# Gate products from the residual rows, with the norm's weight in the gate matrix and its row factor on the difference of the logits

## The reference

```python
x = o @ wo + residual
residual = x
h = rmsnorm(x, ff_ln_w)            # x * rsqrt(mean(x*x) + eps) * w
ht = h.reshape(-1, Dx)
logits = ht @ gate_w               # 256 x 8
top_vals, top_idx = jax.lax.top_k(logits, K)      # K = 2
gates = jax.nn.softmax(top_vals, axis=-1)
for e in range(E):                 # E = 8
    we = jnp.sum(gates * (top_idx == e), axis=-1)
    ye = jax.nn.silu(ht @ w1[e]) * (ht @ w3[e]) @ w2[e]
    out = out + we[:, None] * ye
```

## Time and profile before

| | us |
|---|---|
| median of three runs | 618.45 |
| lowest, highest | 615.74, 618.65 |
| profiled execution | 618.01 |
| its span | 616.2 |
| TensorE busy | 504.7 (82%) |
| VectorE busy | 499.4 (81%) |
| ScalarE busy | 362.0 (59%) |
| POOL busy | 242.5 (39%) |

### The profile page before, as it was taken

The page is one execution under the profiler, slowest core; times in us unless marked ns, Lnnn a source line. Parts: engine busy times, 40 slices in busy tenths (PEclk is TensorE's granted clock), DMA queues, the critical chain, the costliest instruction groups (busy, mean ns, idle before and its releaser), DMA issues.

```text
span 616.2 us, 10966 instructions
## 1 busy us (share of the span) xinstructions
PE 504.7 (82%) x3893; PEld 408.5 (66%) x3893; DVE 499.4 (81%) x978; ACT 362.0 (59%) x769; POOL 242.5 (39%) x208
## 2 busy tenths in 40 slices
PE   2017766799999999999669999999999999357893
PEld 1002323478788878888448999999999999223462
DVE  4999986599988888886638979989999899458894
ACT  3344435588887778776217556574565455437772
POOL 3253245644444445540653185442333510360012
PEclk9999888899999999999979999999999999788897
DMA  8300004000230000000269798899769751130001
GB/s 257 150 1 0 1 0 136 2 2 2 77 104 2 2 1 10 27 1 2 70 244 361 273 330 197 275 280 322 272 244 337 283 108 69 51 104 0 8 25 38
DMA packets 36531, 71.87 MB, mean 117 GB/s; under 512 B 5276, under 2 KB 21916, under 8 KB 36220
## 3 DMA queue, kind: packets, MB, share of 16 engines
q10 hardware_dynamic: 15280, 40.77, 20.0%
q1 hardware_dynamic: 18123, 22.26, 10.7%
q0 software_dynamic: 3072, 8.14, 5.2%
HBM read 66.03 MB, written 5.12 MB: 115 GB/s over the span
## 4 chain that ended last, share of the span: by engine, by line
PE 49%; DVE 30%; issue 7%; ACT 6%; DMA 3%; another core or an unknown queue 2%; SPq 1%; ACTq 1%; POOL 0%; DVEq 0%; POOLq 0%
PE pb L454 10%; PE pw L454 8%; PE sc L520 6%; PE pt L706 5%; PE po L454 5%; PE pb L706 4%; PE sc L706 4%; PE pt L531 3%; DVE areg L1341 2%; DVE areg L1723 2%; DVE areg L1325 2%; DVE areg L1323 2%; DVE areg L1312 1%; DVE rs L1779 1%
## 5 line engine op out<-in xcount | busy, mean ns | idle before, releaser
L1929 POOL TENSOR_TENSOR breg<-breg,con 128x512 f32<-128x512 f32 x36 | 46.9, 1302 | 89.6 <-ACT breg L956 89.6
L454 PE MATMUL pb<-areg,wreg 128*128 128x512 f16 x240 | 63.5, 406 | 14.3 <-ACT breg L956 13.0
L964 ACT ACTIVATE breg<-breg,mx 128x128 f32<-128x128 f32 (+1 forms) x128 | 56.7, 447 | 3.2 <-DVE mx L1467 3.2
L454 PE MATMUL pw<-areg 128*128 128x256 f16 x406 | 56.5, 273 | 1.4 <-DVE areg L1730 1.4
L1115 ACT CAST areg<-areg 128x512 f16<-128x512 f32 (+1 forms) x46 | 25.9, 565 | 49.3 <-DVE areg L1716 46.8
L706 PE MATMUL pb<-areg,wreg 128*128 128x128 f32 x448 | 52.7, 275 | 0.6 <-issue 0.6
L706 PEld LDWEIGHTS pb<-areg,wreg 128*128 128x128 f32 x448 | 51.3, 192 | 0.9 <-issue 0.8
L454 PEld LDWEIGHTS pb<-areg,wreg 128*128 128x128 f16 x240 | 22.9, 102 | 42.7 <-ACT breg L956 14.2
L706 PE MATMUL pt<-areg,wreg 128*128 128x128 f32 x424 | 49.9, 275 | 1.3 <-DMA wreg<-in_L_ffn_w 1.3
L706 PEld LDWEIGHTS pt<-areg,wreg 128*128 128x128 f32 x424 | 48.5, 192 | 1.6 <-DMA wreg<-in_L_ffn_w 1.5
L706 PE MATMUL sc<-areg,wreg 128*128 128x128 f32 x416 | 49.0, 275 | 0.0
(11 more groups left out here) (261 smaller groups left out, 1262.9 us busy)
## 6 DMA issues: line engine op xcount, KB each, us to landing
wreg<-in_L_ffn_w ACTq DMA_DIRECT2D x40, 896.0 KB
wreg<-in_L_ffn_w SPq DMA_DIRECT2D x14, 896.0 KB
ys_dram<-areg ACTq DMA_DIRECT2D x23, 128.0 KB
wreg<-in_L_ffn_wq SPq DMA_DIRECT2D x1, 2048.0 KB, 8.9
wreg<-in_L_ffn_wo SPq DMA_DIRECT2D x1, 2048.0 KB, 8.1
areg<-in_fside_BxSxS ACTq DMA_DIRECT2D x4, 256.0 KB, 5.7
x_in<-in_x SPq DMA_DIRECT2D x4, 256.0 KB, 4.3
h_dram<-areg SPq DMA_DIRECT2D x8, 128.0 KB
```

The lines of the kernel that those rows point to most:

```text
L454: last = nc.tensor.matmul(bank, w(a), m(b), start=first and k == 0, stop=final and k == 2)
L964: last = nc.scalar.activation(pr[:, parity, b, o:o + w], pr[:, parity, b, o:o + w], ACT.Exp, bias=mx[:, parity, k:k + 1], scale=-1.0, accu ...
L1929: G.tensor_tensor(t2[:, parity, :].rearrange("p (b n) -> p b n", b=2), t2[:, parity, :].rearrange("p (b n) -> p b n", b=2), rope_sin.rearr ...
```

## The change

The gate products are made from the residual rows. Per row, the norm is a positive factor; it is left out of the logits, whose order it doesn't change, and multiplied into the difference of the two largest before the exponential. The norm's weight per feature is multiplied into the gate matrix once, in step 16 of attention, from a new load `fflnc` at the start. The normalised rows, which only the experts still need, are made beside: for tiles 4 to 7 by ScalarE (row factor) and POOL (weight), in place of VectorE; for tiles 0 to 3 as before. The squares of tiles 4 to 7 stand behind the copies. The transposes of tiles 0 to 3 move one step earlier, and their copies with them; ten filler matmuls become four. The three VectorE instructions for the gate values stand behind the row numbers. Half of POOL's gathers of gate rows go behind its first two tile gathers.

```diff
+                sp.dma_start(fflnc[:, :], t["L0_ffn_ff_ln_w"].rearrange("(c p) -> p c", p=P)).then_inc(s["norm_in"], 16)
...
             def route_transposes(i):
-                pe.wait_ge(s["h2_ready"], i + 1)
+                pe.wait_ge(s["x1a_done"], i // 2 + 1)
...
-                    last = nc.tensor.transpose(route_bank(i)[:, c * P:(c + 1) * P], h2[:, i, c * P:(c + 1) * P], ident)
+                    last = nc.tensor.transpose(route_bank(i)[:, c * P:(c + 1) * P], x0[:, i, c * P:(c + 1) * P], ident)
...
+                if QU + 1 <= u < QU + 5:
+                    route_transposes(u - QU - 1)
                 if u >= QU + 2:
-                    route_transposes(u - QU - 2)
-                if u >= QU + 3:
-                    route_products(u - QU - 3)
+                    route_products(u - QU - 2)
...
-            route_products(NT // 2 - 1)
-            keep_clock(pt2[:, 1, :], 10)
+            keep_clock(pt2[:, 1, :], 4)
...
-                if u >= QU + 2:
-                    copy_h2T(u - QU - 2)
+                if u == H:
+                    for c in range(C):
+                        nc.scalar.activation(gate_w[:, c, :], gate_w[:, c, :], ACT.Copy, scale=fflnc[:, c:c + 1]).then_inc(s["gate_folded"], 1)
+                if QU + 1 <= u < QU + 5:
+                    copy_h2T(u - QU - 1)
...
+            for i in range(NT // 2, NT):
+                copy_h2T(i)
             for i in range(NT // 2, NT):
                 squares_of_tile(i)
             for i in range(NT // 2, NT):
-                copy_h2T(i)
+                act.wait_ge(s["rstd2_ready"], i // 2 + 1)
+                nc.scalar.activation(h2[:, i, :], x0[:, i, :], ACT.Copy, scale=ssq[:, 2, i:i + 1]).then_inc(s["h2_scaled"], 1)
...
-            for i in range(4, NT):
-                second_norm(i)
...
-            dve.sem_inc(s["d_ready"], 1)
-
-            dve.wait_ge(s["ge_ready"], 1)
-            link(V.tensor_scalar(gts[:, :, 2], gts[:, :, 1], 1.0, None, ALU.add))
-            link(V.reciprocal(gts[:, :, 3], gts[:, :, 2]))
-            link(V.tensor_tensor(gts[:, :, 4], gts[:, :, 3], gts[:, :, 1], ALU.mult))
+
+            dve.wait_ge(s["rstd2_ready"], NT // 2)
+            V.tensor_tensor(gts[:, :, 0], gts[:, :, 0], ssq[:, 2, :], ALU.mult).then_inc(s["d_ready"], 1)
...
+            dve.wait_ge(s["ge_ready"], 1)
+            link(V.tensor_scalar(gts[:, :, 2], gts[:, :, 1], 1.0, None, ALU.add))
+            link(V.reciprocal(gts[:, :, 3], gts[:, :, 2]))
+            link(V.tensor_tensor(gts[:, :, 4], gts[:, :, 3], gts[:, :, 1], ALU.mult))
...
-            gather_rows("L1_ffn_w_gate")
+            pool.wait_ge(s["norm_in"], 64)
+            pool.wait_ge(s["h2_ready"], 4)
+            for i in range(4, NT):
+                pool.wait_ge(s["h2_scaled"], i - 3)
+                G.tensor_tensor(h2[:, i, :], h2[:, i, :], ffln[:, :], ALU.mult).then_inc(s["h2_ready"], 1)
+            gather_rows("L1_ffn_w_gate", 0, NI // 2)
...
-            gather_tiles(0, 1, 2, 3)
+            gather_tiles(0, 1)
+            gather_rows("L1_ffn_w_gate", NI // 2, NI)
+            gather_tiles(2, 3)
```

More of the change, by code:

```diff
@@ L169, in build @@
         ffln = sb("ffln", [P, D])
+        fflnc = sb("fflnc", [P, C])
         wu = sb("wu", [P, 4, C])
@@ L466, in _ @@
             pe.wait_ge(s["con_in"], 16)
-            pe.wait_ge(s["norm_in"], 48)
+            pe.wait_ge(s["norm_in"], 64)
             pe.wait_ge(s["hlo_done"], 2)
@@ L566, in route_products @@
                     pe.wait_ge(s["max_done"], QU)
+                    pe.wait_ge(s["gate_folded"], C)
                 for c in range(C):
@@ L944, in hidden_high @@
                 last.then_inc(s["hi_done"], 1)
-            act.wait_ge(s["norm_in"], 48)
+            act.wait_ge(s["norm_in"], 64)
             HH = HD // 2
@@ L1974, in _, with gather_rows @@
             pool.wait_ge(s["didx_in"], 16)
-            def gather_rows(name):
-                for c in range(NI):
+            def gather_rows(name, first, last):
+                for c in range(first, last):
                     G.indirect_dma_start(out=rows[0:IQ, c * D:(c + 1) * D], out_offset=None, in_=t[name],
@@ L2008, in _ @@
             pool.wait_ge(s["rq_ready"], 1)
-            gather_rows("L1_ffn_w_up")
+            gather_rows("L1_ffn_w_up", 0, NI)
             gather_tiles(7, 8)
```

4 lines of the change are left out of this document (2 added, 2 removed).

## The result

| | before | after |
|---|---|---|
| median of 12 runs, us | 619.10 | 622.36 |
| lowest, highest | 615.74, 620.78 | 620.31, 627.02 |
| span of the profiled execution | 616.2 | 620.5 |
| ratio to before, 95% interval | | 1.0067 (1.0047 to 1.0088) |

The change is slower: 0.67% by the ratio of the runs, 3.3 us between the two medians. The forecast was 617.6 in 613.7 to 621.6.

The account below looks back on a forecast made before the run. TensorE and VectorE, busy four fifths of 616.2 us, were taken to bound it through a chain of waits. Terms -1.86 + 1.0 + 0.3 = -0.56 gave 617.45 from 618.01, or 617.9 by the median; forecast 617.6, range 613.7 to 621.6.

Parts of the forecast that it names:

- End of attention: Last head unit: ScalarE's earlier copy delays the exponentials 0.95, and the last output projection ends 0.57 late.
- Gate products: Tiles 4 to 7: no wait for the norm and fewer fillers start transposes 1.86 earlier, the 0.57 delay included.
- the clock of the rival: Rival: with fewer fillers TensorE falls to the 0.50 clock for the four-tile ladder, 3.3 more, 620.9; chance 0.05.
- Gate values and normalised rows beside: Router: moving tiny instructions taken as 0, root factors in time with 0.6 to spare, nobody waits for the stored rows.
- The lock: Router chain: POOL's multiplies block VectorE's two-input instructions through shared ports; cost taken as 1.0, bounds 0 and 3.2.
- Three collisions at half a multiply, 0.35 each: Router chain: how the cost of POOL's multiplies to VectorE was sized, 1.05, taken as 1.0.
- Gathers moved: Start of the expert stage: gate-row gathers behind tile gathers cost 0.3, within bounds 0 and 3.3.
- I take 0.3, since both have slack of about that size: Expert stage: the cost taken for weights landing later and POOL's recurrence parts moving later together.
- 0.9 at most: Second expert tile: delay of the expert weights' load by 0.36 MB more moving beside it at 408 GB/s.
- recurrence parts holding VectorE's work: Expert stage: POOL's recurrence parts, moved later to end about 327, hold VectorE's two-input work, up to 2.4.
- waits whose releaser the profile does not know: Rival: unexplained waits, ScalarE's at 362.82 and VectorE's at 546.73, may go or come: 613.9 or 621; chance 0.17.
- POOL becomes the bound: Rival: POOL from 301.4 to 328 stops the mask chain, holds VectorE's work and delays weights, 622.7; chance 0.13.

Follow-up runs that it names:

- rows_early: Changed kernel with four gate-row gathers issued at the end of attention, the other four ahead of the tile gathers; 618.73 us, ratio 0.9989 to the kernel before.
- thin_rows: Changed kernel whose second four gate-row gathers take 8 rows each instead of 88, the rest left out; 619.31 us, one execution.
- y_pause: `folded` with POOL waiting after eight of the 16 gathers of experts' results for VectorE's first dense scale; 615.08 us, ratio 0.9924 to the kernel before.
- broken_run: Changed kernel with POOL's 3.9 us recurrence arithmetic moved between the second gate-row gathers and tile gather 2; 625.91 us, ratio 1.0115 to the kernel before.
- before_again: The kernel before, unchanged, run once more for a second profile; 613.40 us, one execution.
- folded: `rows_early` without POOL's multiplies, the norm's weight multiplied in ScalarE's copy of the gathered tiles; 617.33 us, ratio 0.9977 to the kernel before.
- after_again: The changed kernel, unaltered, run once more for a second profile; 623.19 us, one execution.

## Why the prediction was wrong, point by point

*End of attention.* Right in kind, a little small: +0.85 for +0.57 (the copy ahead of the exponentials). The part for the subtraction itself, 284.48 to 285.4, was close; that TensorE would win back 0.35 of it by the end of attention was not so.

*Gate products.* Right. Predicted 1.86 earlier with the 0.57 in it; measured 2.34 less 0.85, 1.49. The ladder had the same length in both profiles, though in the second the granted clock was 0.83 in 298 to 300 and 0.50 in 300 to 302, so the clock of the rival did fall there, and cost the ladder nothing.

*Gate values and normalised rows beside.* Right: L1569 took 0.16 and had its root factors in time, and the first tile gather waited for row numbers.

*The lock.* Right in mechanism, mis-sized. The step that failed is "Three collisions at half a multiply, 0.35 each": the chain met four multiplies back to back, and each of four mask instructions lasted one whole multiply. The first three cost 1.57; the fourth, the mask sum, cost 0.47 in the stretch of the ranks. I had the multiplies start 2.46 behind the logits' copy and counted only L1560 of these four. That was wrong even by my own times, by which L1558 and L1559 also start behind 301.4 (at 301.45 and 301.58); only L1557, at 301.31, lies ahead. The multiplies started 2.26 behind the copy, ahead of L1563 at 2.37. And there was a part that I did not price: in the first profile TensorE, idle for 3.47, was at the lower clock for the ranks, 0.43 more; in the second it was not. Together 2.0 to 2.5 for 1.0. The rule of the Trainium skill that I cited (the loser fully blocks) fits each of the four instructions, and I should have summed by it.

*Gathers moved.* The step that failed most: "I take 0.3, since both have slack of about that size", where 2.5 to 2.7 were paid. Its size lay within my bounds (0 and 3.3). The slack was not there: the load of the second expert's weights ended a wait before the change already, and with four of the gathers at the end of attention instead (`rows_early`) both the SiLU (8.76) and the second expert's first product (12.92) are back where they were. Two things showed. One I did not have at all: with eight gathers in a row on POOL, ScalarE's first SiLU starts only 1.5 to 2 us after the last, and the split alone does it to the kernel before. The other I had priced at "0.9 at most" and then all but dropped: with 8 rows for 88 the SiLU is as late, but that product starts some 1 us earlier (14.11 for 14.96 to 15.53). How the loss divides between the two is open. Of recurrence parts holding VectorE's work no profile showed anything. I had the clue in hand as a rival, "waits whose releaser the profile does not know", and gave it a place at 362 and 546 only, without asking what POOL was doing at those times.

The sum by the measured terms, first two stretches to the first SiLU: +0.85 - 2.34 + 1.57 + 0.90 + 2.73 = +3.7 for -0.56, and by the second pair of profiles 3.4, against 3.3 between the medians. That the sums agree so well is in part luck: stretches behind the first SiLU vary by 1 us and more between executions of one kernel. The rival *POOL becomes the bound* named the right engine, stretch and direction at 622.7, and had 0.13; its condition on the masks held, the 0.9 for the weights is near what `thin_rows` won back, and the rest of its price came by another way: so its number was near by luck. What stays open: the stretch behind the experts is 2.3 and 2.8 longer after than before in the two pairs of profiles, but 17.7 to 23.5 over all kernels that did not touch it; whether the change has a share in it the runs don't tell. Nor do they tell what in POOL's issuing holds the others: the held instructions had their data, the engine's own wait names nothing, and for the first SiLU the four gate gathers' traffic is excluded. All held ones (first SiLU of a stage, first dense product) were new pieces of the program, which would fit a supply of instructions that is cut off, but that is argued and not shown. The DMA queue of instructions in the profiles speaks against its simplest form for the first SiLU: in `thin_rows` its only transfer from 310 on starts between 321 and 322, and none follows until after the SiLU's start at 325.37; the profile of after has one at the same place and its SiLU at 325.27.

## What to carry to other kernels

Count how many indirect gathers POOL issues without a break, and what new piece of work another engine starts under them; try to split the run where POOL would wait anyway (`rows_early`, `y_pause`). A break that makes a needed gather late cost more than it won (`broken_run`). And ask what each moved gather's bytes travel beside: a load that already ends a wait has no slack. Before moving an elementwise product to POOL, list VectorE's two-input instructions that fall beside it: here each lasted as long as a whole POOL instruction, however small it was, and in one execution of two TensorE, waiting for them, lost its clock as well. A per-feature factor may ride in a copy from PSUM that ScalarE makes anyhow: here the two halves with the factor took 0.62 for 0.37, and the tiles were no longer.

## What the runs showed of the hardware that was not expected

- Runs of eight and sixteen indirect gathers on POOL (0.95 us each, 0.30 apart) went with waits of ScalarE and VectorE that mostly have no releaser in the profile; behind a run of eight ScalarE's first SiLU started 1.5 to 2.0 us after its end. Gathers of 8 rows did it as those of 88 did. In the run of 16, gaps of 0.39 us changed nothing, and with one of 6.67 us the waits were gone. There VectorE's product started anywhere from 3.5 us before the run's end (547.76 and 551.22 in `before_again`) to 2.6 after it, so its tie to the run is looser. The third such wait, 3.54 at 362.82, lies inside a run of gathers too; it is missing in the second profile of the same kernel, and it was not tried.
- A two-input VectorE instruction of 128 x 8 took 0.71 beside POOL multiplies of 0.69, as did those of 128 x 64.
- One indirect gather took 3.33 and 3.31 in place of 0.98 beside a 2.34 us pair of two-input VectorE instructions; smaller ones (128x64, 0.23) beside gathers slowed neither (`folded`, 300.4 to 304.4).
- TensorE's clock was at the lower level for the ranks after 3.47 us of idle time, and not after the 1.42 of before or the 1.91 of `after_again`. The idle time alone doesn't explain it: in `after_again` the clock was at 0.50 in 300 to 302, while fillers ran, and at 1.00 in 303 to 305, behind the idle time.
